# Global attention: the turned row maxima copied out of PSUM by ScalarE between two exponentials, and counted by a semaphore of their own

## What is computed

```python
def _L0_attn_ref(x, w_qkv, w_out):
    N_HEADS = 16
    ...
    B, L, D = x.shape                      # 4, 1024, 256
    H = N_HEADS
    Dh = D // H                            # 16
    qkv = jnp.einsum('bld,ed->ble', x, w_qkv)
    q, k, v = jnp.split(qkv, 3, axis=-1)
    ...
    q = _rope(q)
    k = _rope(k)
    scale = 1.0 / jnp.sqrt(jnp.asarray(Dh, dtype=x.dtype))
    scores = jnp.einsum('blhd,bmhd->bhlm', q, k) * scale
    attn = jax.nn.softmax(scores, axis=-1)
    out = jnp.einsum('bhlm,bmhd->blhd', attn, v).reshape(B, L, D)
    return jnp.einsum('bld,ed->ble', out, w_out)

x = L0_attn_x
xn = _layernorm(x, axis=-1)
s = _L0_attn_ref(xn, L0_attn_w_qkv, L0_attn_w_out)
g = _silu(_L0_ffn_ref(xn, L0_ffn_wqkv, L0_ffn_q_scale, L0_ffn_k_scale, L0_ffn_wo, L0_ffn_ln_g, L0_ffn_ln_b,
                       L0_ffn_w1, L0_ffn_b1, L0_ffn_w2, L0_ffn_b2))
x = x + s * g
```

## Time and profile before

| what | us |
|---|---|
| median of 3 runs (lowest, highest) | 2305.58 (2305.26, 2310.74) |
| the profiled execution | 2310.06 |
| its span | 2308.3 |
| busy: TensorE matmuls, VectorE, ScalarE | 2197.8, 1620.2, 1375.1 |

### The profile page before, as it was taken

The page is one execution under the profiler, slowest core; times in us unless marked ns, Lnnn a source line. Parts: engine busy times, 40 slices in busy tenths (PEclk is TensorE's granted clock), DMA queues, the critical chain, the costliest instruction groups (busy, mean ns, idle before and its releaser), DMA issues.

```text
span 2308.3 us, 43409 instructions
## 1 busy us (share of the span) xinstructions
PE 2197.8 (95%) x14592; PEld 1287.6 (56%) x14592; DVE 1620.2 (70%) x3785; ACT 1375.1 (60%) x2547; POOL 614.2 (27%) x493
## 2 busy tenths in 40 slices
PE   7869999999999987989999999999999999999998
PEld 4533333334333335656766766756766766766755
DVE  5767999999999936666566665656666665655635
ACT  2214888888888864645655645645655645655633
POOL 4521300000000005423333333323333233333302
PEclk9975999999999998999999999999999999999999
DMA  4575111122211112210000000000010000000122
GB/s 139 181 236 173 57 57 57 56 66 66 66 47 57 43 63 94 95 37 1 1 0 0 0 0 0 27 1 1 9 37 1 1 0 0 0 0 0 55 92 73
DMA packets 76984, 108.96 MB, mean 47 GB/s; under 512 B 14204, under 2 KB 49360, under 8 KB 76752
## 3 DMA queue, kind: packets, MB, share of 16 engines
q1 hardware_dynamic: 76864, 107.30, 14.6%
HBM read 68.74 MB, written 43.95 MB: 49 GB/s over the span
## 4 chain that ended last, share of the span: by engine, by line
PE 51%; DVE 2%; issue 1%; ACT 1%; DVEq 0%; ACTq 0%
PE ffn L1199 24%; PE l_ps_o L1157 5%; PE ring L1145 5%; PE ring L1185 4%; PE ps_v L1132 3%; PE ps_q L1132 3%; PE ps_k L1132 2%; PE ring L1169 2%; PE ring L1187 1%; DVE l_probs L1675 1%; PE ring L1188 0%; ACT k_ring L1481 0%; DVE l_probs L1687 0%; ACT l_probs L1489 0%; PE ps_k L1221 0%
## 5 line engine op out<-in xcount | busy, mean ns | idle before, releaser
L669 DVE TENSOR_REDUCE maxima<-ps_m 128x1 f32<-128x512 f32 x1024 | 629.7, 683 | 30.7 <-PE ps_m L549 26.7
L737 ACT ACTIVATE probs<-ps_st 128x1024 f32<-128x1024 f32 x512 | 521.0, 1025 | 172.0 <-PE ps_st L576 152.8
L549 PE MATMUL ps_m<-k_st,q_st 48*128 48x512 f32 x1024 | 398.2, 472 | 19.8 <-DMA k_st<-ks 15.6
L576 PE MATMUL ps_st<-q_st,k_st 50*128 50x512 f32 x1024 | 373.3, 450 | 2.3 <-DMA q_st<-max_rows 1.9
L1489 ACT ACTIVATE l_probs<-l_probs,l_neg_max 128x256 f32<-128x256 f32 x512 | 254.0, 498 | 194.8 <-DVE l_neg_max L1675 194.8
L592 PE MATMUL ps_o<-probs,v_st 128*32 128x256 f32 x4096 | 327.4, 398 | 0.1
L1675 DVE CUSTOM_DVE_ANT_1 l_probs<-ring,l_mask 128x256 f32<-128x256 f32 x384 | 140.1, 421 | 198.5 <-PE ring L1185 198.0
L576 PEld LDWEIGHTS ps_st<-q_st,k_st 50*128 50x128 f32 x1024 | 157.2, 189 | 198.4 <-issue 176.5
L1468 ACT COPY p_turned<-ring 128x512 f32<-128x512 f32 x256 | 140.4, 599 | 163.7 <-PE ring L1145 163.5
L1094 POOL TENSOR_SCALAR clipped<-sumsq 128x16 f32<-128x16 f32 x64 | 16.1, 252 | 765.7 <-DVE sumsq L1642 765.7
L549 PEld LDWEIGHTS ps_m<-k_st,q_st 48*128 48x128 f32 x1024 | 169.4, 193 | 53.0 <-DVE maxima L669 31.3
(11 more groups left out here) (192 smaller groups left out, 3879.7 us busy)
## 6 DMA issues: line engine op xcount, KB each, us to landing
qs<-split SPq DMA_DIRECT2D x16, 512.0 KB, 3.5
ks<-split SPq DMA_DIRECT2D x16, 512.0 KB, 5.1
q_st<-qs SPq DMA_DIRECT2D x64, 128.0 KB, 2.5
k_st<-ks SPq DMA_DIRECT2D x64, 128.0 KB, 3.2
o<-o_sb SPq DMA_DIRECT2D x32, 256.0 KB, 2.4
hidden<-o SPq DMA_DIRECT2D x17, 256.0 KB, 6.5
x_in<-in_L_attn_x_dram SPq DMA_DIRECT2D x8, 512.0 KB, 5.6
v<-v_sb SPq DMA_DIRECT2D x16, 256.0 KB, 4.7
```

Source lines behind the costliest of these rows:

```text
L549: nc.tensor.matmul(bank(base, use)[:, :], q_st[u][r, qt * P:(qt + 1) * P], k_st[u][r, h * CH:(h + 1) * CH], start=True, stop=True).then_in ...
L576: mm = nc.tensor.matmul(ps_st[j][:, h * CH:(h + 1) * CH], k_st[u][r, kt * P:(kt + 1) * P], q_st[u][r, h * CH:(h + 1) * CH], start=True, st ...
L669: nc.vector.tensor_reduce(maxima[:, par, side(e), tile + e // 4, e % 2:e % 2 + 1], bank(base, k + e)[:, :], AX_X, ALU.max).then_inc(m_used, 1)
L737: nc.scalar.activation(probs[:, kt % 4, j, :], ps_st[j][:, :], ACT.Exp, scale=float(G_DIM) ** -0.5).then_inc(exp_done, 1)
```

## The change

take_rows, the copy of the turned maxima from the ring to max_rows, moves from VectorE to ScalarE. There it stands right behind the exponential of (kt 6, j 0) in each unit but the last, and, for unit 0, ahead of all exponentials. It no longer counts into m_used but into a semaphore of its own, rows_copied. With it the counts change: a unit has 33 uses (USES) but 32 reads in m_used (TAKEN). bank_free, which now takes the unit, waits on rows_copied where the use three earlier was the transpose, and otherwise on m_used with the transpose left out of the count. place_rows on SP and split_maxima on POOL wait on rows_copied, and turned_at becomes turned_use. The matmuls, the reductions, the exponentials and the DMAs are the same and in the same order.

```diff
--- before.py
+++ after.py
+        rows_copied = sem("rows_copied")
...
+        TAKEN, LEAD_TAKEN = USES - 1, LEAD - 1
...
-        def turned_at(n):
+        def turned_use(n):
-            if isinstance(n, int) and n == 0:
+            if n < 0:
                 return 2 * HALF
-            return LEAD + USES * (n - 1) + (HALF if isinstance(n, int) and n == UNITS - 1 else TURNED)
+            return HALF if n == UNITS - 2 else TURNED
...
                 def place_rows(i, u):
-                    sp.wait_ge(m_used, turned_at(NB * i + u) + 1)
+                    sp.wait_ge(rows_copied, NB * i + u + 1)
...
                     pool.wait_ge(max_found, n + 1)
                     if not isinstance(n, int) or n:
-                        pool.wait_ge(m_used, turned_at(n - 1) + 1)
+                        pool.wait_ge(rows_copied, n)
...
-                def bank_free(base, use):
-                    if not isinstance(base, int) or base + use >= M_BANKS:
-                        pe.wait_ge(m_used, base + use + 1 - M_BANKS)
-
-                def maxima_scores(base, use, u, qt, j, h):
-                    bank_free(base, use)
+                def bank_free(n, use):
+                    ahead, turned = use - M_BANKS, turned_use(n)
+                    start = LEAD_TAKEN + TAKEN * n if n >= 0 else 0
+                    if ahead == turned:
+                        pe.wait_ge(rows_copied, n + 2)
+                    elif start + ahead >= 0:
+                        pe.wait_ge(m_used, start + ahead + (ahead < turned))
+
+                def maxima_scores(n, use, u, qt, j, h):
+                    bank_free(n, use)
+                    base = LEAD + USES * n if n >= 0 else 0
...
-                def take_rows(base, use, i, u):
-
-                    dve.wait_ge(m_ready, base + use + 1)
-
-                    if u:
-                        dve.wait_ge(rows_in[u - 1], 32 * i + 32)
-                    elif not isinstance(i, int) or i:
-                        dve.wait_ge(rows_in[NB - 1], 32 * i)
-                    nc.vector.tensor_copy(max_rows[:, :], bank(base, use)[0:4 * TILES, 0:P]).then_inc(m_used, 1)
...
-                            join_maxima(n + 1, (u + 1) % 2, base + HALF)
+                            join_maxima(n + 1, (u + 1) % 2, LEAD_TAKEN + TAKEN * n + HALF)
                         if more2:
                             take_maxima(base, HALF, u % 2, 0, range(2, TURNED - HALF))
-                        if more1:
-                            take_rows(base, TURNED if more2 else HALF, i if u + 1 < NB else i + 1, (u + 1) % NB)
-                        if more2:
                             take_maxima(base, HALF + 1, u % 2, 0, range(TURNED - HALF, HALF))
...
             def _(act):
+                def take_rows(ready, turned, i, u):
+
+                    act.wait_ge(m_ready, ready)
+
+                    if u:
+                        act.wait_ge(rows_in[u - 1], 32 * i + 32)
+                    elif not isinstance(i, int) or i:
+                        act.wait_ge(rows_in[NB - 1], 32 * i)
+                    nc.scalar.copy(max_rows[:, :], turned[0:4 * TILES, 0:P]).then_inc(rows_copied, 1)
...
                                 nc.scalar.activation(probs[:, kt % 4, j, :], ps_st[j][:, :], ACT.Exp,
                                                      scale=float(G_DIM) ** -0.5).then_inc(exp_done, 1)
+                                if (kt, j) == (TURN, 0) and not (last and u == NB - 1):
+                                    use = HALF if last and u == NB - 2 else TURNED
+                                    base = LEAD + USES * n
+                                    take_rows(base + use + 1, bank(base, use), i if u + 1 < NB else i + 1, (u + 1) % NB)
                                 if (kt, j) == (0, 1):
...
                     act.wait_ge(stored[c], 16 * STORES * B)
+                take_rows(2 * HALF + 1, bank(0, 2 * HALF), 0, 0)
                 body(0, True, False)
```

More of the change, by code:

```diff
@@ L555, in operands_in, with half_maxima, turn_maxima @@
                     pe.wait_ge(qk_in[u], LOADS * i + LOADS)
-                def half_maxima(base, k, i, u, half):
+                def half_maxima(n, k, i, u, half):
                     if half == 0:
                         operands_in(i, u)
-                    for n in range(HALF):
-                        maxima_scores(base, k + n, u, 4 * half + n // 4, side(n), n % 2)
-                def turn_maxima(n, base, use):
+                    for e in range(HALF):
+                        maxima_scores(n, k + e, u, 4 * half + e // 4, side(e), e % 2)
+                def turn_maxima(n, use):
                     pe.wait_ge(split_done, n + 1)
-                    bank_free(base, use)
+                    bank_free(n - 1, use)
+                    base = LEAD + USES * (n - 1) if n else 0
                     nc.tensor.transpose(bank(base, use)[0:4 * TILES, 0:P], max_hl[:, :, :, :].rearrange("p a b c -> p (a b c)").bitcast(F32),
@@ L620, in body @@
                         n = NB * i + u
-                        base = LEAD + USES * n
                         i1, u1 = (i, u + 1) if u + 1 < NB else (i + 1, 0)
@@ L636, in body @@
                             if kt == TURN and more1:
-                                turn_maxima(n + 1, base, TURNED if more2 else HALF)
+                                turn_maxima(n + 1, turned_use(n))
                             for h in range(2):
@@ L640, in body @@
                                 if m:
-                                    maxima_scores(base, *m[h])
+                                    maxima_scores(n, *m[h])
                             second_half(i, n, kt, u, first)
@@ L645, in body @@
                                 if m:
-                                    maxima_scores(base, *m[2 + h])
+                                    maxima_scores(n, *m[2 + h])
                             first_half(i, n, kt, u, first)
@@ L653, in _ @@
                 for half in range(2):
-                    half_maxima(0, HALF * half, 0, 0, half)
+                    half_maxima(-1, HALF * half, 0, 0, half)
                 pe.wait_ge(ident_loaded, 16)
-                turn_maxima(0, 0, 2 * HALF)
-                half_maxima(0, USES, 0, 1, 0)
+                turn_maxima(0, 2 * HALF)
+                half_maxima(-1, USES, 0, 1, 0)
                 body(0, True, False)
@@ L712, in _ @@
                 join_maxima(0, 0, 2 * HALF)
-                take_rows(0, 2 * HALF, 0, 0)
                 take_maxima(0, USES, 1, 0, range(HALF))
```

## The result

The changed kernel takes 2322.27 us, median of 13 runs (2316.89 to 2342.31), against 2305.58 for the kernel before (13 runs, 2300.71 to 2311.64): 16.7 us or 0.7% slower by the medians; the ratio is 1.0084, with a 95% interval of 1.0061 to 1.0108. 2324.8 had been predicted. Measured once more (c1_change_again) the ratio is 1.0064 (1.0040 to 1.0089), 2321.81 against 2305.74.

What follows compares the result with a forecast made beforehand. TensorE was taken as the bound, by 0.03 us per half-step. Removing VectorE's copy gives 0; waits for ScalarE's copy add 29 x 0.65 + 0.33 = 19.2 us to the median 2305.58, giving 2324.8 us, range 2319 to 2334.

Steps and rivals of the forecast that it cites:

- The bound: Global attention: TensorE sets the pace at 1.23 us per half-step, VectorE close behind at 1.20 us per pair of reductions.
- The removal: VectorE's copy of the turned maxima disappears in each unit; VectorE waits for TensorE's next maxima instead, so worth 0.
- The path of the wait: TensorE's weight load waits for ScalarE's copy, which stands behind the exponential of (6, 0): 0.65 us late per unit.
- use 27: First maxima matmul of key tile 6's second half-step, in the turned maxima's bank; weight load predicted at 441.43, before 440.78.
- The terms: Copy starts 0.92 us after the exponential's start, takes 0.27 us, and releasing the bank costs about 0.05 us.
- The count: Of 32 transposes, 29 units pay 0.65 us each, unit 0 pays 0.33; unit 30 and the first transpose pay 0.
- The sum: Whole kernel: 29 x 0.65 + 0.33 = 19.2 us added, giving 2324.8 us on the median.
- main case: TensorE waits for ScalarE's copy in each unit; 16.8 to 27.0 us added, 2322.4 to 2332.6; chance 0.83.
- The rows' DMA: Rival: row DMAs issued later on SP land late for the next unit's scores; at most 24 us, 2349; chance 0.05.
- The clock: Rival: unit 0's new 0.33 us pause keeps the clock at half one unit longer, 7 us, 2332; chance 0.04.
- VectorE as the bound: Rival: VectorE sets TensorE's pace, so 31 copies less give back 7.4 us, 2298.2; chance 0.03.
- no change: Rival: later matmuls on TensorE catch up, or the copy does not wait for the exponential; 2306; chance 0.05.

Runs made afterwards that it cites:

- e4_dve_twice_moved: Kernel before with the turned maxima copied twice on VectorE and 30 tiny fills ahead of its loop; ratio 0.9997, 590.6 us from unit 1 to unit 30.
- e1_copy_ahead: Changed kernel with ScalarE's copy ahead of the exponential of (6, 0), not behind it; ratio 0.9994 to the kernel before, 590.6 us from unit 1 to 30.
- e7_wait_alone_moved: Kernel before, VectorE's copy counting into rows_copied, TensorE also waiting for the exponential of (6, 0), 30 fills ahead of VectorE's loop; ratio 1.0075, 606.2 us unit 1 to 30.

## Why the prediction was right, point by point

**The bound.** TensorE was the bound and VectorE followed: shown by e4_dve_twice_moved (0.24 us more per unit on VectorE, nothing lost) and e1_copy_ahead (its copy gone, nothing gained). The removal was rightly booked at 0. The size of the margin, 0.03 us per half-step, is a reading of the earlier trace rows; the runs show only that VectorE has at least those 0.24 us per unit to spare.

**The path of the wait.** Exponential, copy, bank, use 27: each step is in the timeline where it was put, and e1_copy_ahead takes the wait away and the cost with it, while e7_wait_alone_moved puts it in without the copy. This is shown, not argued.

**The terms.** The copy started 0.92 us behind the exponential's start, as taken from the pair in the earlier trace rows. It took 0.24 us, where the line through 377 and 587 ns in the earlier trace rows gave 0.27; the estimate of 250 ns, from the Trainium skill's page "VectorE: DVE Perf Modes", section on the TRN2 errata, was the closer one, and the measurement, 239 ns, lies below both. The release took 0.05. The weight load was late by 0.62 us where 0.65 was predicted, and unit to unit it is 0.64; where in the unit the other 0.02 arise was not looked for.

**The count.** That all of the 29 units pay the same was wrong by a little. The times came from a unit in the loops. Outside them (units 1 to 3, 28 and 29) ScalarE's exponential starts 0.98 us behind the transpose (258.72 to 259.70) and not 1.06, and a unit pays 0.55. Unit 0 paid 0.31, for 0.33.

**The sum.** 19.2 us were predicted and 18.3 are in the trace (18.0 + 0.3), 16.7 between the medians, with an interval that reaches from 14 to 25. The sum was 5% too high against the trace, 0.9 us: 0.65 was put in where a unit in the loops pays 0.64, and five units start the copy 0.08 us earlier. The medians' 16.7 lies just under the 16.8 that the prediction gave as the least of its main case, and inside its range; the trace's 18.3 lies inside both. The medians of whole executions can't tell 16.7 from 18.3: the clock's rise alone makes 6 us between two executions of one kernel. What the difference comes from stays open.

**The rivals.** The rows' DMA was not late: the issue moved to 491.77 and the next unit's start waits for nothing. The clock did not stay at half longer because of the new pause. Both profiled executions have unit 0 at half clock, and the rise falls into these windows (first the kernel before, then the changed one, granted clock third from the end):

```profile
217.00:225.00 8.00, 8.00 (x48) 3.15 (x48) 4.54 (x8) 4.33 (x5) 0.00 (x0) 0.55 0.38 116
```

```profile
225.00:229.00 4.00, 4.00 (x34) 2.03 (x28) 2.80 (x5) 2.81 (x4) 0.00 (x0) 0.79 0.22 83
```

The rise comes 15.3 us behind unit 0's transpose before and 15.8 us behind it now, and unit 0 as a whole is 0.31 us longer, which is the wait and nothing more. In c1_change_again the clock was full before unit 0's pause, and stayed so. What brings the rise the runs don't show: in the kernel before TensorE was busy for all of 195 to 209 us and for 8.00 of the next 8 at a granted clock of 0.50. VectorE as the bound fell (e1_copy_ahead), and so did no change.

**What I had expected to see.** Among the waits I had foretold a line of 16 to 19 us behind ScalarE's copy; it says 10.4, since the view counts idle time of the weight loads and not lateness. VectorE's idle time was to rise by the delay and its 0.24; it rose from 12.6 us to 30.7, 0.75 us per unit, since the reduction behind the copy's old place waits 0.16 us and not 0.24. The pace of the units was the right measure.

**Not foreseen.** The fetch of VectorE's code was in no step and no rival: of the new counts the prediction said only that no instruction is added on TensorE. The changed kernel did not meet it (38 packets on that queue, as before), and that was luck. Its loop is 8 instructions shorter and also lies elsewhere; which of the two spared it was not tested. Had the copy's counts been taken apart without moving the copy, the edit would have cost 30 us for a reason that no row of the kernel before shows.

## What to carry to other kernels

Where a ring of buffers is read by two engines, a slot comes free only when the second engine has done all that stands ahead of the read in its own order. Put the read ahead of the long instruction and not behind it, if its input is there by then. The place of four lines decides 18 us here, and on which of the two engines the copy runs decides nothing. Before moving work off a busy engine, double that work in an experiment: if nothing is lost, that engine is not the bound, and taking work off it gains nothing. And when an edit that should cost nothing costs much, compare the packets of the instruction queues and look for an engine that idles on "issue" behind a loop's branch.

## What the runs showed of the hardware

- A loop on VectorE of 278 instructions ran without stops. With 4 instructions more in it, or with 4 more ahead of it, VectorE stopped for 2.1 to 2.8 us behind each of its five branches back, and the instruction queue had 63 or 64 packets for 38. With 30 more ahead of the loop of 282 the stops were gone (39 packets).
- A stop of VectorE of 2.56 us, around which TensorE was busy for 4.06 of 6 us, was followed by a granted clock of 0.66 over 10 us, and in that run passes were up to 9.3 us longer than without.
- ScalarE's copy of 32x128 out of PSUM takes 239 ns, and ScalarE's next instruction starts 0.10 us ahead of the end of the one before, for exponential to copy (490.58 + 1.02, 491.50) as for copy to copy (449.14 + 0.24, 449.28).
- A weight load started 0.05 us behind the end of the copy that released it (one semaphore to wait for), and another 0.11 us behind the end of the exponential that released it (two semaphores). What makes the difference was not tested.
- The clock's rise in the first units came at times at least 15 us apart in two executions of the same kernel (full from 209 us in one, half until after 225 in the other), worth 5.9 us.
